# Edge pass with a stacked gate network and its numbers in PSUM; tally passes with fp32 one-hots

## The reference, cut to what matters

```python
gate = silu(edge_attr @ F1W + F1b) @ F2W + F2b                  # 40 -> 48 -> 48, per edge
gate = gate + (emb[z[src]] * (emb[z[dst]] @ adapt)).sum(-1)
cw   = where(d < 6, 0.5 * (cos(pi * d / 6) + 1), 0)
msg  = gate * h[dst] * (cw * mult[dst])
agg, tot = segment_sum(msg, src), segment_sum(mult[dst], src)
...
out2 = segment_sum(x[row] * norm, col)                          # third layer
out3 = segment_sum(x[row] * norm, col)                          # fourth, with self loops
```

## Time and profile before

| | |
|---|---|
| three runs | 16614.99, 16660.92 (median), 16723.33 us |
| profiled execution | 16637.34 us, its span 16635.7 us |
| busy | PE 58%, weight loads 46%, DVE 67%, ACT 32%, POOL 56% |
| mean granted clock of TensorE | 0.733 |
| `edge_keys` | about 91 to 2472 us of the span |
| `edge_pass` | 2472 to 5274 us |
| the two `tally` passes | 14870 to 15522 us and 15886 to 16542 us |

### The profile page before, as it was taken

One profiled execution on the slowest core, in us unless ns is written; L12 is line 12 of the kernel. 1 busy time (PEld: TensorE's weight loads), 2 busy tenths in 40 slices (PEclk: granted clock), 3 DMA queues, 4 the chain that ended last, 5 costly groups with the idle time before them and its releaser, 6 DMA issues. The chain is left out here.

```text
span 16635.7 us, 392824 instructions
## 1 busy us (share of the span) xinstructions
PE 9596.0 (58%) x115995; PEld 7636.4 (46%) x115995; DVE 11221.7 (67%) x27173; ACT 5368.0 (32%) x15471; POOL 9241.3 (56%) x11101
## 2 busy tenths in 40 slices
PE   2011008888885338975896599569926666543332
PEld 1011005444543037864885588468824444343332
DVE  6985006666665567985897599759954455369788
ACT  0000003333331015652663266336613433322222
POOL 7888777666665714431442244124427777637365
PEclk9855555555555569988997799789967878775765
DMA  3522335555556237644663566266622222262532
GB/s 109 176 71 80 98 101 102 102 102 103 102 101 69 53 108 215 175 127 173 181 174 89 203 174 175 64 234 175 174 58 62 62 66 63 49 201 71 144 112 54
DMA packets 1458570, 1976.56 MB, mean 119 GB/s; under 512 B 411908, under 2 KB 1125764, under 8 KB 1451465
## 3 DMA queue, kind: packets, MB, share of 16 engines
q1 hardware_dynamic: 1074622, 1326.66, 25.5%
q0 software_dynamic: 309216, 511.82, 18.0%
q10 hardware_dynamic: 74552, 135.95, 2.5%
HBM read 1245.74 MB, written 614.07 MB: 112 GB/s over the span
## 5 line engine op out<-in xcount | busy, mean ns | idle before, releaser
L681 POOL DMA_INDIRECT attend_rows<-key_rows,attend_fetch_now x1824 | 1749.2, 959 | 2060.2 <-PE attend_seg L1717 1732.5
L1761 ACT ACTIVATE attend_hot<-attend_lane_hot,attend_share 128x128 f32<-128x128 fp8e4 x7296 | 2228.6, 388 | 1244.6 <-DVE attend_share L1784 1213.4
L681 POOL DMA_INDIRECT edges_rows<-raw,edges_perm_now x1824 | 1866.6, 1023 | 883.9 <-issue 782.1
L681 POOL DMA_INDIRECT keys_rows<-table,keys_staged x1564 | 1848.4, 1182 | 470.7 <-issue 470.7
L1717 PE MATMUL attend_seg<-attend_rows,attend_hot 128*128 128x49 f32 x14592 | 1821.2, 279 | 126.2 <-ACT parts_layer L1765 83.5
L1717 PEld LDWEIGHTS attend_seg<-attend_rows,attend_hot 128*128 128x128 f32 x14592 | 1738.9, 196 | 211.8 <-issue 209.5
L681 POOL DMA_INDIRECT mlp_xin<-table,mlp_staged x1564 | 1510.4, 966 | 473.1 <-issue 472.5
L1088 PE MATMUL edges_ps_t<-ident,edges_attr 128*40 128x128 f32 x1824 | 427.8, 413 | 1433.7 <-ACT edges_attr L1137 1433.7
L681 POOL DMA_INDIRECT tally_rows<-rows_by_source,tally_origin_now x912 | 977.6, 1072 | 299.7 <-issue 234.0
L1704 PE MATMUL attend_qx<-attend_table,attend_oht 128*128 128x90 bf16 x21888 | 1098.5, 208 | 67.2 <-DMA attend_oht<-src_hots 65.0
L1801 DVE TENSOR_REDUCE attend_mraw<-attend_top 128x2 f32<-128x1024 f32 x912 | 1110.4, 1218 | 16.2 <-PE attend_top L1737 12.4
(11 more groups left out here) (543 smaller groups left out, 23436.7 us busy)
## 6 DMA issues: line engine op xcount, KB each, us to landing
key_rows<-expand_out SPq DMA_DIRECT2D x304, 624.0 KB
attend_ea<-edge_attrs SPq DMA_DIRECT2D x912, 160.0 KB
attend_table<-q SPq DMA_DIRECT2D x1832, 67.5 KB
expand_oht<-dst_hots SPq DMA_DIRECT2D x304, 384.0 KB, 3.9
attend_oht<-src_hots SPq DMA_DIRECT2D x912, 128.0 KB
attend_lane_hot<-src_hots_by_edge SPq DMA_DIRECT2D x912, 128.0 KB
raw<-keys_rows ACTq DMA_DIRECT2D x46, 2176.0 KB
rows_by_source<-spread_out SPq DMA_DIRECT2D x152, 576.0 KB, 4.8
```

Source lines behind the costliest of these rows:

```text
L681: return nc.gpsimd.indirect_dma_start(out=out, out_offset=None, in_=table, in_offset=bass.IndirectOffsetOnAxis(ap=index, axis=0))
L1761: ins = nc.scalar.activation(hot[p][:, u, c, :], lane_hot8[r][:, u, c, :], ACT.Copy, scale=share[p][:, u, c:c + 1])
```

## The change

Three edits. In `edge_keys` and `edge_pass` a copy of `k.iota` is put in PSUM once and is the second operand of the comparisons. In `edge_pass` pairs of columns go through the gate network together: the weights lie twice, as blocks on the diagonal, so there are 4 transposes of 80 columns, one product with `w1` (80 rows, 512 columns), 4 products with `w2` (97 rows, 96 columns), and ScalarE copies and Silus half the elements per partition on twice the partitions. Its engines are also put in another order: ScalarE starts its step with table, transposed attributes and gate of earlier steps, then takes the attributes of step n, then Silu and Sin of n-1; TensorE does the one-hot products last; `val3` is double; VectorE adds up the sums of step n-3, and does so between the one-hots of L1202 and the wait of L1206. In `tally` the gathered fp32 rows go into the matmul as they are, against fp32 one-hots, 48 columns a matmul; the split in parts goes away; ScalarE copies the sums out of PSUM; lane numbers lie in PSUM.

```diff
 edge_keys
+        numbers = turned[:, 0:P]
+            ch.step(v.tensor_copy(numbers, k.iota[:]))
...
-                    v.tensor_tensor(hot[b][0], bc(blk[0][:, here], NT), rows_of(k.iota[:, 0:NT], C), ALU.is_equal)
+                    v.tensor_tensor(hot[b][0], bc(blk[0][:, here], NT), rows_of(numbers[:, 0:NT], C), ALU.is_equal)
...
-                    v.tensor_tensor(lane_hot[b], bc(loc[1][:, here], P), rows_of(k.iota[:], HC), ALU.is_equal)
+                    v.tensor_tensor(lane_hot[b], bc(loc[1][:, here], P), rows_of(numbers, HC), ALU.is_equal)
 edge_pass
+        val3 = [ph.sb(f"val3{b}", [P, COL, 3, RW], BF16) for b in two]
+        w1, w2, b1 = ph.sb("w1", [2 * RBF, 2 * F]), ph.sb("w2", [2 * F + 1, 2 * F]), ph.sb("b1", [2 * F, 1])
+        PAIR = GR // 2
+        eT, act1 = ph.sb("eT", [2 * RBF, CHR * PAIR, P]), ph.sb("act1", [2 * F + 1, CHR * PAIR, P])
+        numbers = ph.ps("numbers", [P, 512])[:, 0:P]
 TensorE
+                        for c in range(PAIR):
+                            ins = nc.tensor.transpose(ps_t[0:2 * RBF, u * PAIR + c, :], attr[p][:, u, c * 2 * RBF:(c + 1) * 2 * RBF], k.ident[:])
...
+                    for c in range(CHR * PAIR):
+                        ins = mm(ps_2[:, c * 2 * F:(c + 1) * 2 * F], act1[:, c, :], w2[:], start=True, stop=True)
...
+                    mm(ps_1[0:2 * F].rearrange("p c g -> p (c g)"), w1[:], eT[:].rearrange("p c g -> p (c g)"), start=True, stop=True).then_inc(s_1, 1)
+                if live(n, 2):
...
+                            ins = mm(ps_s[:, u * (3 * RW):(u + 1) * (3 * RW)], hot_s8[p][:, u * GR + c, :], val3[p][:, u * GR + c].rearrange("p j w -> p (j w)"),
+                                     start=(c == 0), stop=(c == GR - 1))
 ScalarE
+                if live(n, 1):
+                    act.wait_ge(s_dl, n)
+                    act.sem_inc(s_taken, 1)
+                    after(act, s_exp, n - 2)
...
+                        ins = a(table[1 - p][:, u], k.emb3[:, :, bass.ds(block_i * G, G)], ACT.Copy)
...
+                    act.wait_ge(s_t, n)
+                    a(eT[:], ps_t[0:2 * RBF], ACT.Copy).then_inc(s_tc, 1)
+                if live(n, 2):
+                    act.wait_ge(s_2, n - 1)
+                    a(gate[p][:], ps_2[:, 0:COL * F].rearrange("p (c f) -> p c f", f=F), ACT.Copy).then_inc(s_2c, 1)
...
 VectorE
+                if live(n, 3):
+                    dve.wait_ge(s_seg, n - 2)
+                    v.tensor_reduce(k.parts[:, bass.ds((n - 3) * (CHR * RW), CHR * RW)].rearrange("p (u w) -> p u w", u=CHR),
...
-                    ch.step(v.tensor_tensor(hot_s8[o], bc(r[:, :, SL], P), rows_of(k.iota[:], COL), ALU.is_equal, saturate=False))
+                    ch.step(v.tensor_tensor(hot_s8[o], bc(r[:, :, SL], P), rows_of(numbers, COL), ALU.is_equal, saturate=False))
 tally
-        hot = [ph.sb(f"hot{b}", [P, EX * GR, P], BF16) for b in two]
-        parts3 = [ph.sb(f"parts3{b}", [P, EX * GR, 3, F], BF16) for b in two]
+        hot = [ph.sb(f"hot{b}", [P, EX * GR, P]) for b in two]
...
-                pe.wait_ge(s_low, n + 1)
+                pe.wait_ge(s_rows[r], (t + 1) * (16 * EX))
+                pe.wait_ge(s_hot, n + 1)
...
+                        ins = nc.tensor.matmul(ps[b][:, u, :], hot[b][:, u * GR + c, :], rows[r][:, u, c * F:(c + 1) * F],
+                                               start=(c == 0), stop=(c == GR - 1))
...
-                nc.scalar.activation(parts3[b][:, :, 0, :], rest[r], ACT.Copy).then_inc(s_high, 1)
-                nc.scalar.activation(parts3[b][:, :, 1, :], rest[r], ACT.Copy).then_inc(s_mid, 1)
+                act.wait_ge(s_seg, n + 1)
+                nc.scalar.activation(k.parts[:, bass.ds(n * (EX * F), EX * F)].rearrange("p (u f) -> p u f", f=F), ps[b], ACT.Copy).then_inc(s_ev, 1)
...
-                v.tensor_tensor(rest[r], rest[r], parts3[b][:, :, 0, :], ALU.subtract).then_inc(s_rest, 1)
-                v.tensor_tensor(parts3[b][:, :, 2, :], rest[r], parts3[b][:, :, 1, :], ALU.subtract).then_inc(s_low, 1)
```

More of the change, by code:

```diff
@@ L1036, in _ @@
             sp.wait_ge(s_ones, 1)
[L1037 to L1040, removed]
+            for q in two:
+                f = slice(q * F, (q + 1) * F)
+                sp.dma_start(w1[q * RBF:(q + 1) * RBF, f], i["L0_gnn_F1W"]).then_inc(s_w, 16)
+                sp.dma_start(w2[f, f], i["L0_gnn_F2W"]).then_inc(s_w, 16)
+                sp.dma_start(w2[2 * F:2 * F + 1, f], i["L0_gnn_F2b"].rearrange("(a n) -> a n", a=1)).then_inc(s_w, 16)
+                sp.dma_start(b1[f, :], column(i["L0_gnn_F1b"])).then_inc(s_w, 16)
             def step(n, s, t):
@@ L1135, in step @@
                     after(act, s_kept[p], halves(s, t) * 32)
+                    after(act, s_t, n - 1)
                     a(wt[p][:], rows[b][:, :, WT], ACT.Copy)
@@ L1138, in step @@
                     a(k.dl_a[:, bass.ds(n * COL, COL)], rows[b][:, :, DL], ACT.Copy).then_inc(s_dl, 1)
[L1139 to L1149, removed]
-                if live(n, 1):
-                    act.wait_ge(s_2, n)
-                    a(gate[1 - p][:], ps_2[:, 0:COL * F].rearrange("p (c f) -> p c f", f=F), ACT.Copy).then_inc(s_2c, 1)
-                if live(n, 0):
-                    act.wait_ge(s_1, n + 1)
-                    a(act1[0:F], ps_1[0:F], ACT.Silu, bias=b1[:]).then_inc(s_1a, 1)
-                    after(act, s_seen, n - 1)
-                    act.wait_ge(s_arg, n + 1)
-                    a(cw[p][:], phase_[p][:], ACT.Sin, bias=half[:], scale=-np.pi / 6.0).then_inc(s_cos, 1)
-            steps(act, step, 1)
+                if live(n, 1):
+                    act.wait_ge(s_1, n)
+                    a(act1[0:2 * F], ps_1[0:2 * F], ACT.Silu, bias=b1[:]).then_inc(s_1a, 1)
+                    after(act, s_seen, n - 2)
+                    act.wait_ge(s_arg, n)
+                    a(cw[1 - p][:], phase_[1 - p][:], ACT.Sin, bias=half[:], scale=-np.pi / 6.0).then_inc(s_cos, 1)
+            steps(act, step, 2)
         @block.vector
@@ L1168, in _ @@
             v.memset(k.dl_a[:, NS * GR:], 255.0)
+            ch.step(v.memset(w1[:], 0.0))
+            ch.step(v.memset(w2[:], 0.0))
+            ch.step(v.tensor_copy(numbers, k.iota[:]))
             ch.done(v.memset(act1[:], 1.0))
@@ L1223, in step @@
                     dve.sem_inc(s_seen, 1)
-                    split(v, ch, val[:], [val3[:, :, j, :] for j in range(3)], rest[:])
+                    split(v, ch, val[:], [val3[o][:, :, j, :] for j in range(3)], rest[:])
                     dve.sem_inc(s_val, 1)
-                if live(n, 2):
-                    dve.wait_ge(s_seg, n - 1)
-                    v.tensor_reduce(k.parts[:, bass.ds((n - 2) * (CHR * RW), CHR * RW)].rearrange("p (u w) -> p u w", u=CHR),
-                                    ps_s[:, 0:CHR * 3 * RW].rearrange("p (u j w) -> p u w j", u=CHR, j=3), AX, ALU.add).then_inc(s_ev, 1)
             for s in range(TURN):
@@ L1239, in _ @@
             ch.n, ch.base = n0 + (LOOPS - 1) * per, 0
-            for s in range(2):
+            for s in range(3):
                 step(CHN + s, s, LOOPS)
@@ L2525, in step @@
                 pool.wait_ge(s_now, n + 1)
-                after(pool, s_low, n - RINGS + 1)
+                after(pool, s_seg, n - RINGS + 1)
                 pool.sem_inc(s_pool_turn, 1)
```

71 lines of the change are left out of this document (25 added, 46 removed).

## The result

The changed kernel takes 16422.09 us (median of 4 runs, 16405.03 to 16448.95), beside 16651.91 us for the kernel before (4 runs): ratio 0.9858, 95% interval [0.9822, 0.9894]. The forecast was 16430 us and 1.4% less.

What follows compares the result with a forecast made beforehand. GpSimd bounds `edge_keys`; the half-clock TensorE-to-ScalarE chain and GpSimd alternate in the edge pass. 16637.3 - 200 - 312 + 3 + 280 = 16408 us profiled, scaled to 16430, 1.4% less; range 16250 to 16680, the forecast's own 16250 to 16640.

Steps and rivals of the forecast that it cites:

- `edge_keys`, -200: Both counting loops: with a PSUM operand gathers return to 0.944 us, taking 200 us off; bounds nothing and 206.
- third rival: `edge_keys` and edge pass: the PSUM operand frees nothing; 16760 us, slower by 0.6%; chance 0.09.
- Edge pass, -309: Edge pass: step falls from 12.17 to 10.8 us over 228 steps, -312, with +3 for start and end.
- 8 x 1.25 = 10.0: Edge pass: GpSimd's eight gathers a step at 1.25 us each, part of its 10.4 us bound.
- collisions: Edge pass: gathers lengthened by VectorE, 0.64 us a step before, taken as 0.4 after.
- waits: Edge pass: GpSimd's idle time beyond its usual 0.30 us before a gather, 0.41 us a step.
- wait of 0.71 us once a step: Edge pass, sign of being right: GpSimd idle 0.30 us before a gather, but 0.71 once a step.
- new engine order: Edge pass: reduction moves into VectorE's wait, Silu of n-1 leaves the chain before attributes of n; VectorE's period 10.3 us.
- first rival: Edge pass: a chain over TensorE and VectorE keeps the step at 12.17 us; 16745 us, slower; chance 0.14.
- Tally, +280: Both tally passes: TensorE becomes the bound, 48 fp32 rows, 10.3 us a step, 1588 us against 1308.
- second rival: Tally: TensorE gets full clock, GpSimd binds, 1170 us for both passes, -138 instead of +280; 16010 us; chance 0.06.
- Everything else, 0: Phases outside `edge_keys`, edge pass and tally: predicted to change by 0 us.

Runs made afterwards that it cites:

- e1: The kernel before with only the `edge_keys` comparison numbers moved to PSUM; 16451.7 us, ratio 0.9885.
- e8: The changed kernel with the edge pass's lane comparison reading its numbers from SBUF again; 16521.94 us, edge pass 2645.7 us.
- e7: The changed kernel with each stacked `w2` product of the edge pass issued twice; 16431.91 us, edge pass 2524.9 us.
- e9: The changed kernel with the edge pass in the old engine order, one `val3` and sums two steps late; 16401.51 us, edge pass 2543.7 us.
- e6: The changed kernel with nine unread bf16 products of 512 columns in a burst ahead of each tally step's matmuls; 16014.43 us.
- e3: The kernel before with the new `tally` alone; 16927.65 us, ratio 1.0165.
- e10: The changed kernel with the unstacked edge pass of before, only its comparison numbers in PSUM; 16708.18 us, edge pass 2802.9 us.

## Why the prediction was right, point by point

- **`edge_keys`, -200, measured -198.** Gathers at 0.95 us in both loops; e1 shows it alone. The third rival (the second operand's place frees nothing) is out: e1 for `edge_keys`, e8 for the edge pass, where it had priced the place at 130 us and 106 were measured.
- **Edge pass, -309, measured -263.** The bound was named rightly: GpSimd, with its usual idle time of 0.30 us before 1791 of 1823 gathers; more work on TensorE costs nothing (e7), and longer gathers cost nearly all that they are longer (e8). Two sizes were off. The present step of 12.17 us was read from a window of 2761 us that ended at 5247, but the last gather starts at 5221.4: 25 us with no gathers in it were counted as steps. From first to last gather it is 12.05 us, so 0.12 x 228 = 27 us of the gain were never there. And the new step came out at 10.91 us instead of 10.8, another 25 us. The two together, 52 us, are the gap between -312 and -263 but for 3 us; from the last gather to the end of the phase it is some 50 us in both. The new step term by term: 8 x 1.25 = 10.0 held. For collisions I took 0.4 us a step; they are (1.016 - 0.944) x 8 = 0.58, hardly less than the 0.64 of before. For waits I took 0.41; they are 0.34, and that they come so near is luck: the wait of 0.71 us once a step, named as a sign, did not show, and 54 of the 78 us are the three long waits at the end of the phase. Without them the step is the median's 10.56 us.
- **Where the collisions went.** Counted over the traces by what VectorE runs when a gather starts, the gathers of before are 145 us longer in sum than 0.944 us each: 63 under L1220, 39 under L1214, 26 under L876. Those of after are 132 us longer. Under the same comparison, now L1230, 127 gathers start and none is longer, as forecast. But in their new rhythm more gathers meet other instructions: 30 us under L1208, 30 under L1224, 28 under L881 (one takes 1.31 us in the timeline above), 20 under L1232, 17 under L1226 (1.13). L1208 is no pair of fp32 tiles: it compares one bf16 tile with a number per partition.
- **The new engine order.** The prediction had it move the reduction into VectorE's wait and take Silu out of the chain. It does (VectorE's period 10.43 us, its wait 0.57 us; predicted 10.3), but VectorE isn't the bound, and e9 is at most 24 us longer without it. The first rival (a chain keeps the step at 12.17) is out.
- **Tally, +280, measured +271.** The step of 10.24 us is 48 rows of 0.213 us; predicted 10.3. The rest, the start of 11 us, was about right: 788.8 - 76 x 10.24 = 11. TensorE at 0.50 through both passes: the Trainium skill, "TensorE: Matmul & The Clock Gate", Part 1, would have an uninterrupted stream earn the full clock, and 778 of 790 us busy did not. The second rival (full clock) didn't come by itself; its price was right, though: 1170 us for both passes, and e6 with the clock brought back takes 1194 with more work in it. The prediction named no bound for the tally of before. It was GpSimd: no gather there has more than its usual 0.30 us of idle time before it, and a gather takes 1.07 us on the mean, 0.95 after. So the edit did take the collisions away, and put TensorE in GpSimd's place.
- **Which pairs collide.** The prediction counts L2577 among the fp32 pairs and has L2579, bf16 with fp32, spare the gather. Both readings fail. By the kernel the second operand of L2577 is a bf16 part, and its gather of 2.09 us is late all the same. Of the 441 gathers that start under an L2579, 217 start within 0.01 us of its start and the others in its last 0.12 us, where by the last section below nothing is added; so these rows show no pair that is spared. The first kind may hold up VectorE instead, whose instruction then takes 0.72 us and not 0.68. The sum does not hang on this, with TensorE as the bound.
- **Everything else, 0, measured -25.** The four attention passes took 1039.4, 1041.3, 1040.7 and 1039.3 us before and 1031.1, 1027.7, 1029.5 and 1027.4 after, 45 us less with the same code; other phases took some 20 us more. In e3, where `edge_keys` and the edge pass are those of before, they take 1035 to 1042, in the other runs 1025 to 1038. The cause was not looked for and is open.
- **The sum.** 16430 forecast and 16422 measured is nearer than the terms were, by luck: the edge pass gained 46 us less than forecast, while the tally lost 9 less and everything else came out 25 shorter. The range's lower end, 16250, does not follow from its terms: 16661 - 206 - 403 + 280 is 16332.

## What to carry to other kernels

Before you price a step, take its period from the first and the last instruction of the bound engine, not from a window whose ends you chose. A VectorE comparison with two fp32 operands in SBUF holds up GpSimd's gathers (2.97 us instead of 0.95 beside L631); moving the constant one to PSUM costs a copy or two and pays only where GpSimd is the bound, 198 us in `edge_keys`, 106 us in the stacked edge pass, nothing in the unstacked one. Leaving out a split in bf16 parts is no gain by itself: two fp32 rows with 128 weight columns each and few moving ones can cost more than one bf16 product and the split together (789 against 652 us a pass) while TensorE is granted 0.50 of its clock, so look at the granted clock and not at the number of instructions.

## What the runs showed of the hardware

- TensorE was busy 778 of 790 us, without a gap, and granted 0.50 all the time, in both passes, its work being fp32 matmuls of 128 weight and 48 moving columns. With nine bf16 products of 512 columns a step in one burst it was granted 0.93, with four 0.50, with eight spread evenly 0.51 and 0.57.
- Where its clock is up, TensorE gives an fp32 row in 5.45 / 48 = 0.114 us, at the lower level in 0.213. With 96 moving columns instead of 48 a row of the `w2` products costs 1.03 / 8 = 0.129 us at the higher level, about as much as those of before with 48 (2.13 / 16 = 0.133 in e10's edge pass, at a granted 0.92). So the moving columns don't set it here; that the weight load does is not shown by a run of its own.
- VectorE reads the numbers from PSUM as fast as from SBUF: 2.42 us for 2176 elements both ways, 1.21 and 1.22 for 1024.
- A gather that starts while VectorE is under way with two tiles of SBUF is longer by what is left of that instruction, less 0.126 us (within 0.02 us for all 89 under L631, all 125 under L1220 and 90 of 92 under L1226). By rows 3: L631 ends at 1204.98, 2.15 us after the gather starts, and the gather takes 2.97 - 0.94 = 2.03 us more. The same holds for all 130 under L1208, a `tensor_scalar` from one bf16 tile to fp8. With the second tile in PSUM no gather is longer by more than 0.03 us, wherever it starts (170 under L634, 127 under L1230). So a collision costs what is left of the instruction: the longest ones are the first to move.
